# First mixture-of-experts layer: inputs scaled by GpSimd before the transpose, y copied by ScalarE

## The reference, cut to what matters

```python
x = x + _L0_xattn_ref(...)
x = x + _L0_ffn_ref(_layernorm(x, axis=-1), ...)     # the changed stage
x = x + _L1_xattn_ref(...)
x = x + _L1_ffn_ref(...)

def _moe(x, gate, expert_bias, w1, w2, w3, shared_w1, shared_w2, shared_w3):   # 2048 tokens of 256
    scores = sigmoid(xt @ gate.T)                       # 8 experts
    _, sel = top_k(scores + expert_bias, 2)
    routed = xt[token_idx] * scores_sorted[:, None]     # the input is scaled, not the output
    xb = routed.astype(bfloat16)
    for e in range(8):
        h = silu(xb @ w1e.T) * (xb @ w3e.T)             # bfloat16, 256 -> 128
        out_r += where(expert_ids == e, h @ w2e.T, 0)   # 128 -> 256
    out = shared MLP in float32 (256 -> 128 -> 256) + out_r, added at the token's place
```

## Time and profile before

| | |
|---|---|
| median of 3 runs | 3045.92 us (3044.54 to 3047.83) |
| profiled execution | 3046.2 us |
| its span, first to last instruction | 3044.4 us |
| mean granted TensorE clock | 0.969 of 2.4 GHz |
| TensorE busy over the span | 2863.0 us, 94% |
| VectorE | 2123.6 us, 70% |
| ScalarE | 1976.1 us, 65% |
| GpSimd | 1714.9 us, 56% |

### The profile page before, as it was taken

One profiled execution on the slowest core, in us unless ns is written; L12 is line 12 of the kernel. 1 busy time (PEld: TensorE's weight loads), 2 busy tenths in 40 slices (PEclk: granted clock), 3 DMA queues, 4 the chain that ended last, 5 costly groups with the idle time before them and its releaser, 6 DMA issues. The chain is left out here.

```text
span 3044.4 us, 57941 instructions
## 1 busy us (share of the span) xinstructions
PE 2863.0 (94%) x18455; PEld 2444.7 (80%) x18478; DVE 2123.6 (70%) x4527; ACT 1976.1 (65%) x4903; POOL 1714.9 (56%) x2055
## 2 busy tenths in 40 slices
PE   7989999799999999999999999999999976599798
PEld 5768888688888888888888888888888853388655
DVE  7975445677777777777777777777777769766544
ACT  5656666677777777777777777777777636466211
POOL 6766664456556555555655655655665446466132
PEclk9999999999999999999999999999999978799699
DMA  5456767311111111111111111111111042253510
GB/s 180 135 157 206 206 206 230 125 61 54 41 68 54 41 68 54 41 51 58 54 41 67 54 41 68 54 41 55 54 54 41 1 108 52 85 170 123 177 42 26
DMA packets 254418, 261.82 MB, mean 86 GB/s; under 512 B 12998, under 2 KB 226255, under 8 KB 254128
## 3 DMA queue, kind: packets, MB, share of 16 engines
q1 hardware_dynamic: 234608, 237.38, 24.3%
q10 hardware_dynamic: 17312, 15.73, 1.8%
q0 software_dynamic: 2208, 5.12, 0.6%
HBM read 174.10 MB, written 85.00 MB: 85 GB/s over the span
## 5 line engine op out<-in xcount | busy, mean ns | idle before, releaser
L1027 ACT ACTIVATE w_hi<-ps_t 128x512 fp32r<-128x512 f32 (+2 forms) x1024 | 570.4, 557 | 412.6 <-PE ps_t L1267 409.4
L1097 DVE TENSOR_REDUCE piece_max<-ps_s 128x1 f32<-128x512 f32 (+2 forms) x1024 | 631.5, 622 | 257.1 <-PE ps_s L1254 229.3
L1123 DVE TENSOR_TENSOR w_lo<-ps_t,w_hi 128x512 fp32r<-128x512 f32 (+2 forms) x1024 | 656.4, 641 | 200.6 <-ACT w_hi L1027 184.3
L1287 PE MATMUL ps_o<-w_hi,v_hi 128*128 128x256 f32 (+1 forms) x1856 | 595.5, 321 | 0.0
L1194 POOL TENSOR_SCALAR prob<-prob,inv_sum 128x512 f32<-128x512 f32 (+2 forms) x768 | 479.9, 645 | 194.1 <-DVE inv_sum L1113 194.1
L1289 PE MATMUL ps_o<-w_hi,v_lo 128*128 128x256 f32 (+1 forms) x1856 | 523.1, 282 | 0.0
L1288 PE MATMUL ps_o<-w_lo,v_hi 128*128 128x256 f32 (+1 forms) x1856 | 522.3, 281 | 0.0
L1015 ACT ACTIVATE prob<-ps_s,neg_max 128x512 f32<-128x512 f32 (+2 forms) x768 | 487.7, 635 | 43.6 <-DVE neg_max L1104 35.1
L1267 PE MATMUL ps_t<-ident,prob 128*128 128x128 f32 (+1 forms) x2784 | 515.8, 272 | 0.0
L1249 PE MATMUL ps_s<-k_hi,q_hi 128*128 128x512 f32 (+2 forms) x1024 | 403.7, 394 | 27.7 <-ACT prob L1015 18.4
L1267 PEld LDWEIGHTS ps_t<-ident,prob 128*128 128x128 f32 (+1 forms) x2784 | 359.6, 140 | 52.7 <-issue 0.2
(11 more groups left out here) (283 smaller groups left out, 6225.9 us busy)
## 6 DMA issues: line engine op xcount, KB each, us to landing
v_scratch<-v_out SPq DMA_DIRECT2D x120, 256.0 KB, 3.0
raw_k<-k_scratch SPq DMA_DIRECT2D x32, 960.0 KB, 7.0
raw_v<-v_scratch SPq DMA_DIRECT2D x32, 960.0 KB, 4.7
k_scratch<-k_out SPq DMA_DIRECT2D x104, 256.0 KB, 2.7
q_scratch<-out_t SPq DMA_DIRECT2D x64, 256.0 KB, 2.5
r_all<-r_scratch SPq DMA_DIRECT2D x32, 512.0 KB, 4.3
raw_q<-q_scratch SPq DMA_DIRECT2D x32, 512.0 KB, 5.1
first_prob<-in_ctx_t ACTq DMA_DIRECT2D x50, 256.0 KB, 2.8
```

The costliest lines, as they stand in the source:

```text
L1027: nc.scalar.activation(pt_hi[keys, k % RING, cols], ps_t[keys, k % 2, cols], ACT.Copy).then_inc(hi_done, 1)
L1097: nc.vector.tensor_reduce(piece_max[:, n % 2, p:p + 1], ps_s[:, p, lo - p * PC:hi - p * PC], AX.X, ALU.max).then_inc(max_ready, 1)
L1123: nc.vector.tensor_tensor(pt_lo[keys, k % RING, cols], ps_t[keys, k % 2, cols], pt_hi[keys, k % RING, cols].bitcast(F32), ALU.subtract).th ...
L1287: nc.tensor.matmul(out, v_hi[gi][keys, vs], pt_hi[keys, k % RING, cols], start=blk == (0 if qt else 1), stop=False)
```

## The change

The input is scaled in token layout: GpSimd multiplies the rows of `xn` with the token's weight (a scalar per partition) into `xb` in bf16, TensorE transposes `xb` into a bf16 bank `ps_b`, and VectorE copies that to `xbt`. The transpose, store and broadcast loads of the weights go. To free a bank, `ps_h1` has one bank in place of two. ScalarE copies both halves of y, VectorE none. `hidden` is split into a shared and an expert form, and the passes are interleaved anew.

```diff
-        weight = sb("weight4", [P, E0, NT])
-        weight_t = sb("weight4_t", [P, P])
-        weight_all = sb("weight4_all", [P, E0, TOK])
+        weight = sb("weight4", [P, NT, E0])
+        xb = sb("xb4", [P, 2, GT, D], BF16)
...
-        ps_h1 = psum("ps_h1_4", [P, 2, 512])
+        ps_h1 = psum("ps_h1_4", [P, 512])
...
+        ps_b = psum("ps_b4", [P, 1024], BF16)
+        pair_h1, pair_h3 = (ps_h1[:, :], ps_acc[:, 0, :]), (ps_h3[:, 0, :], ps_h3[:, 1, :])
...
@@ sync
-                sp.wait_ge(weight_copied, 1)
-                sp.dma_start(score_dram, weight_t[:, :]).then_inc(weight_written, 16)
-                sp.wait_ge(weight_written, 16)
-                for i in range(NG):
-                    for e in range(E0):
...
-                        sp.dma_start(weight_all[:, e, i * N:(i + 1) * N], rows.to_broadcast([P, N])).then_inc(row_loaded[e], 16)
@@ gpsimd
-                def inputs(k):
...
-                    for c in range(DC):
-                        nc.gpsimd.tensor_tensor(xbt[:, k % 4, c, :], xt[:, c, cols], weight_all[:, e, cols], ALU.mult).then_inc(xbt_ready, 1)
...
+                def scale(k):
                     i, e = divmod(k, E0)
+                    if k >= 2:
+                        pool.wait_ge(xbt_ready, k - 1)
+                    pool.sem_inc(scale_begun, 1)
+                    for t in range(GT):
+                        tile = i * GT + t
+                        nc.gpsimd.tensor_scalar(xb[:, k % 2, t, :], xn[:, tile, :], weight[:, tile, e:e + 1], 1.0,
+                                                ALU.mult, ALU.mult).then_inc(xb_ready, 1)
+
+                pool.wait_ge(xn_ready, NT)
+                pool.wait_ge(weighted, 1)
                 for k in range(STEPS0):
-                    inputs(k)
+                    scale(k)
@@ scalar
+                exponential(0)
+                copy_h3(0)
+                exponential(1)
+                copy_h3(1)
                 for k in range(STEPS0):
                     inverse(k)
                     if k + 2 < STEPS0:
                         exponential(k + 2)
+                    if k:
+                        copy_y(k - 1, 0)
+                        copy_y(k - 1, 1)
+                    if k + 2 < STEPS0:
                         copy_h3(k + 2)
-                    if k and of_act(k - 1, 1):
-                        copy_y(k - 1, 1)
...
@@ vector
+                def inputs(k):
+
+                    dve.wait_ge(xbt_ready, k + 1)
+                    if k >= 4:
+                        dve.wait_ge(h3_ready, SHARED + k - 3)
+                    nc.vector.tensor_copy(xbt[:, k % 4, :, :], ps_b[:, :].rearrange("p (c n) -> p c n", c=DC)).then_inc(xbt_copied, 1)
...
                 for j in range(SHARED):
                     shared_silu(j)
                     shared_gated(j)
+                    if j >= 2:
+                        inputs(j - 2)
                 copy_h1(0)
+                inputs(2)
                 copy_h1(1)
+                inputs(3)
                 denominator(0)
                 for k in range(STEPS0):
...
-                    if k:
-                        copies_of_y(k - 1)
                     silu(k)
                     gated(k)
-                copies_of_y(STEPS0 - 1)
+                    if k + 4 < STEPS0:
+                        inputs(k + 4)
@@ tensor
+                def inputs(k):
+                    pe.wait_ge(xb_ready, (k + 1) * GT)
+                    if k:
+                        pe.wait_ge(xbt_copied, k)
+                    for c in range(DC):
+                        for t in range(GT):
+                            last = nc.tensor.transpose(ps_b[:, c * N + t * P:c * N + t * P + P], xb[:, k % 2, t, c * P:c * P + P], ident_bf[:, :])
+                    last.then_inc(xbt_ready, 1)
...
+                def hidden(k):
+
+                    pe.wait_ge(xbt_copied, k + 1)
+                    if k:
+                        pe.wait_ge(h1_copied, k)
+                    else:
+                        pe.wait_ge(siluf_ready, SHARED - 1)
+                    for c in range(DC):
+                        last = nc.tensor.matmul(ps_h1[:, :], w_bf[:, 0, k % E0, c * H0:c * H0 + H0], xbt[:, k % 4, c, :], start=c == 0, stop=c == DC - 1)
+                    last.then_inc(h1_ready, 1)
+                    if k >= 2:
+                        pe.wait_ge(h3_copied, k - 1)
+                    else:
+                        pe.wait_ge(actf_ready, SHARED + k - 1)
+                    for c in range(DC):
+                        last = nc.tensor.matmul(ps_h3[:, k % 2, :], w_bf[:, 1, k % E0, c * H0:c * H0 + H0], xbt[:, k % 4, c, :], start=c == 0, stop=c == DC - 1)
+                    last.then_inc(h3_ready, 1)
...
                 pe.wait_ge(sw_loaded, 48)
+                shared_hidden(0)
+                shared_hidden(1)
+                pe.wait_ge(score_exps, 1)
+                shared_hidden(2)
+                inputs(0)
+                shared_hidden(3)
+                inputs(1)
+                pe.wait_ge(w_cast, 3 * E0)
                 hidden(0)
+                inputs(2)
                 hidden(1)
...
+                inputs(3)
                 hidden(2)
...
                 shared_outputs(0)
...
                 for k in range(STEPS0):
                     if k + 3 < STEPS0:
-                        hidden(SHARED + k + 3)
+                        hidden(k + 3)
+                    if k + 4 < STEPS0:
+                        inputs(k + 4)
                     if k % E0 == 1 and k > E0:
                         shared_outputs(k // E0)
                     outputs(k)
```

More of the change, by code:

```diff
@@ L1407, in moe_two_of_eight @@
         silu_ready, act_ready = sem("silu4s"), sem("act4s")
-        y_done, y_by_dve, y_by_act = sem("y4"), sem("y4_by_dve"), sem("y4_by_act")
+        y_done, y_copied = sem("y4"), sem("y4_copied")
         shared_done, summed, x_added = sem("shared4"), sem("summed4"), sem("x4_added")
         PAIRS = NT // 2
[L1412 to L1419, removed]
         with nc.Block() as block:
@@ L1479, in half_tanh, with copy_y @@
                         act.wait_ge(siluf_ready, j - 1)
-                    nc.scalar.activation(tanh[:, j % 2, :], ps_h1[:, j % 2, :], ACT.Tanh, scale=0.5).then_inc(tanh_ready, 1)
+                    nc.scalar.activation(tanh[:, j % 2, :], pair_h1[j % 2], ACT.Tanh, scale=0.5).then_inc(tanh_ready, 1)
+                def copy_y(k, h):
+                    act.wait_ge(y_done, 2 * k + h + 1)
+                    if k:
+                        act.wait_ge(summed, 2 * (k - 1) + h + 1)
+                    nc.scalar.activation(y_bf[:, h, :], ps_y[:, h, :], ACT.Copy).then_inc(y_copied, 1)
                 def exponential(k):
@@ L1563, in shared_silu @@
                         dve.wait_ge(actf_ready, j - 1)
[L1564 removed]
+                    nc.vector.scalar_tensor_tensor(silu_f[:, j % 2, :], tanh[:, j % 2, :], 1.0, pair_h1[j % 2], ALU.add, ALU.mult).then_inc(siluf_ready, 1)
                 def shared_gated(j):
@@ L1576, in copy_h1 @@
                         dve.wait_ge(silu_ready, k - 2)
-                    nc.vector.tensor_scalar(h1_bf[:, k % 3, :], ps_h1[:, k % 2, :], EXP_FLOOR, None, ALU.max).then_inc(h1_copied, 1)
+                    nc.vector.tensor_scalar(h1_bf[:, k % 3, :], ps_h1[:, :], EXP_FLOOR, None, ALU.max).then_inc(h1_copied, 1)
                 def denominator(k):
@@ L1670, in route @@
                     last.then_inc(logits, 1)
-                def hidden(n):
-                    k = n - SHARED
-                    if k >= 0:
-                        pe.wait_ge(xbt_ready, DC * (k + 1))
-                    for m, (ps, done, free_f, free) in enumerate(((ps_h1, h1_ready, siluf_ready, h1_copied), (ps_h3, h3_ready, actf_ready, h3_copied))):
-                        if k >= 2:
-                            pe.wait_ge(free, k - 1)
-                        elif n >= 2:
-                            pe.wait_ge(free_f, n - 1)
-                        for c in range(DC):
-                            if k < 0:
-                                a, b = sw[:, m, c * H0:c * H0 + H0], xt[:, c, n * N:(n + 1) * N]
-                            else:
-                                a, b = w_bf[:, m, k % E0, c * H0:c * H0 + H0], xbt[:, k % 4, c, :]
-                            last = nc.tensor.matmul(ps[:, n % 2, :], a, b, start=c == 0, stop=c == DC - 1)
-                        last.then_inc(done, 1)
+                def inputs(k):
[6 more added lines that the diff above has]
+                    last.then_inc(xbt_ready, 1)
@@ new lines, in shared_hidden @@
+                def shared_hidden(j):
+                    for m, (ps, done, free) in enumerate(((pair_h1, h1_ready, siluf_ready), (pair_h3, h3_ready, actf_ready))):
+                        if j >= 2:
+                            pe.wait_ge(free, j - 1)
+                        for c in range(DC):
```

(2 more changed lines are left out.)

64 lines of the change are left out of this document (14 added, 50 removed).

## The result

The changed kernel takes 3015.11 us in the median of 4 runs (3013.14 to 3016.13), the kernel before 3046.43 (3044.54 to 3047.83): a ratio of 0.9897, 95% interval 0.9882 to 0.9911. The forecast was 3025 in a range of 3014 to 3040. The direction and the range hold, the range narrowly: its lower end was 3014, and one of the four runs lies under it. The gain is 31.3 us where 21.2 were forecast.

What follows compares the result with a forecast made beforehand. VectorE, waiting for GpSimd's instructions, was taken to set the pace. 29 x (4.08 - 3.40) = 19.7 us, minus 1.5 for additions to x, plus 3.0 for the tail, gives 21.2: forecast 3025 us, range 3014 to 3040.

Steps and rivals of the forecast that it cites:

- The bound of before: Stage's loop: VectorE sets the pace, three of its instructions per step waiting for GpSimd; surplus 30 us of 116.
- The pass: Loop step: ScalarE's queue at 3.15 us and the loop through TensorE at 3.13 tie; 3.2 taken at full clock, against 4.08.
- The charge of 1.5 for additions to x: Loop: three add_x of 1.29 us on VectorE, with f32 shared outputs on TensorE, cost 0.5 us each, 1.5 in all.
- the 15% at the low clock: Loop: 15% of it at 1.2 GHz with 4.6 us a step, the rest at 3.2, giving 3.4 us per step.
- Rival (b): Loop through hidden and transposes: the clock stays at 1.2 GHz, 4.6 us a step, time 3060; chance 0.07.
- The start: Before the loop: pass 0 still begins at about 2496, TensorE being in shared products until 2489; gain nothing, bounds 2 either way.
- The tail: After the loop's last h1 copy: 14.7 us now, 11.2 and some 0.3 of handovers after; gain 3, bounds 1 and 5.
- Waits at nothing: Loop: VectorE's waits for GpSimd, at most 0.4 us each, fall into its slack and cost nothing; uncovered, up to 1.2 per step.
- Rival (a): VectorE's copy out of PSUM runs at one element per cycle; loop step 3.9 us, gain 6.7, time 3039; chance 0.12.
- Rival (c): Loop: ScalarE's y copies wait for outputs behind hidden and transposes; a pass costs about 4.0, time 3042; chance 0.08.
- The best case (d): Loop: no low clock, transposes at 0.055 us, an earlier start; 3.12 us a step, gain 31, time 3015; chance 0.10.

Runs made afterwards that it cites:

- the y copies alone: The kernel before with both halves of y copied by ScalarE and nothing else changed; 3029.07 us in one run.
- the quartered products: The kernel before with each GpSimd product of 512 columns done in four of 128, same work and output; 3038.51 us, ratio 0.9975.

## Why the prediction was right or wrong

**The bound of before**: shown. The surplus of 30 us on VectorE comes from GpSimd's instructions in progress; halving their length, at the price of the token's weight, gives 26.2 us of loop, 20.5 of them in VectorE's busy time, and with hardly any GpSimd work the surplus is all but gone.

**The pass.** The full-clock figure of 3.2 (ScalarE 3.15, loop 3.13) against 3.12 measured. ScalarE bounds it, with exponentials 3.156 us apart. The loop through TensorE stands under it at 2.94 in ordinary passes (13 of the 29 in the changed kernel), and at 3.14 with the additions to x counted, so next to it. It was set 0.19 too high, 0.15 of it in the transposes (0.07 and 0.27 taken, 0.056 and 0.22 found). The charge of 1.5 for additions to x was not there to pay: ScalarE has a backlog of 0.95 us when one comes and works through it, with 1.64 us of idle time in the whole loop.

**The step that failed in size** is the 15% at the low clock: it was worth 0.15 x 1.4 x 29 = 6.1 us and the granted clock was 1.00. The low stretches of before went with TensorE's waits of up to 3.9 us: every variant with passes of 3.2 us or less has 0.96 to 1.00 in the loop, the y copies alone with 3.52 have 0.88, the quartered products with 3.47 have 0.95, and the changed kernel with y as before, at 3.44 but with the transposes, 1.00. That the waits lower the clock is read from these together; no run changes the waits alone. Rival (b), the clock held low by transposes, falls with it: eight transposes beside eight 256-column and four 512-column products in a pass leave the clock at full speed. The Trainium skill (TensorE: Matmul & The Clock Gate, Part 4: PE-mode transpose) says that transposes do not count as busy for the gate as matmuls do. The loop at 1.00 neither confirms nor refutes that, as no run here has transposes and little else at this pace.

**The start**: forecast as no gain, 2.1 us found. The reason given (TensorE has the shared products until 2489) was nearly right for the loads, worth at most 1.0, and overlooked that the first hidden products then waited for GpSimd's long products, 1.2 to 1.5 us each.

**The tail**: 3 forecast, 1.4 found; 13.36 us instead of 11.5. The estimate had the last inverse end 6.3 us after the loop's last copy of h1, at 2582.76. It ended 7.6 after it:

```profile
2589.75 0.63 ACT L1493 ACTIVATE inv_bf<-log_den 128x512 bf16<-128x512 f32 x1
```

ScalarE is behind when the loop ends (its last exponential ends at T+2.8, not at +1.4), which the estimate left out; that is 1.3 of the 1.9 us. It also left out the clock of 0.50 in most of the rest.

Together: 21.2 forecast, plus 6.1 for the clock, 2.4 for the pass (0.084 x 29), 1.5 for the additions to x, 2.1 for the start, minus 1.6 for the tail: 31.7, against 31.5 in the stage.

**Waits at nothing**: right in effect, though not by the order assumed. GpSimd's four instructions take 1.88 us, not 1.6, and start at T+2.5, so they reach into the next pass and meet den_bf. It kept 0.12 us a pass and the two others 0.03 each, all in VectorE's slack.

**Rival (a)**, the copy at one element per cycle: out, 688 ns. **Rival (c)**, y waiting for outputs: out, ScalarE has no idle time ahead of y_bf in the loop. **The best case (d)** with 3015 and 3.12 us a pass is what came, and it had a chance of 0.10. That the range holds is in part luck: its lower end stood 1 us under the result, at a case that the forecast thought unlikely.

## What to carry to other kernels

Where VectorE's SBUF instructions show a mean far above their shortest, look for GpSimd instructions beside them before counting VectorE's work. Here their length set nearly every wait, so a cheaper or narrower form on GpSimd can be worth more than work taken off VectorE. A clock below full in a stage whose TensorE waits are long should not be carried over to a version with short passes. And once one engine's queue is the whole bound, relieving it gains only the distance to the second bound. That distance has to be counted over a whole group of passes: in ordinary passes here 0.2 us lay between them, with the additions to x 0.02.

## What was not expected of the hardware

A VectorE instruction did not always get its turn after one GpSimd instruction. Behind products of 128x512 with a start every 1.3 us it waited about one of them (maxima of 1.34 to 1.51 us); beside products of 128x128 whose starts lie 0.42 us apart and whose spans of 0.45 overlap, one den_bf waited 9.4 us. The overlap, or that three of these products in four carry no semaphore update, can't be the whole reason: the same run of products goes on without a gap through the loop, and no VectorE instruction there waited over 0.33 us. What set the one case apart was not tried. It appears in the one profile of that variant; its ten runs (3037.20 to 3039.89) fit a start as late in each. Cutting GpSimd work into pieces can so cost more at one place than it gains in the loop.

The copy of bf16 out of PSUM runs at 0.53 ns per element (419 ns for 512, 688 for 1024), twice the pace of f32 at 1.02. The Trainium skill (VectorE: DVE Perf Modes, the perf-mode tier table) gives a copy with a PSUM operand up to twice the base rate; the trace agrees.
